# The change between two layer kinds of a fused graph network: another order on each engine in the last iterations, and chunk 1 entered inside the first half step

## What is computed

```
h = relu(layernorm(x)); x = x + attention0(h)              # 8 heads, masked by adj
h = relu(layernorm(x)); x = x + (o + layernorm(o)*gamma+beta), o = attention1(h)
h = relu(layernorm(x)); x = x + elu(att @ hw + beta*hw)    # hw = h W, att = softmax(leaky(s1+s2)*adj)
h = relu(layernorm(x)); 3 times:                           # gated recurrence
    a = adj @ h
    z = sigmoid(a W3 + h U3); r = sigmoid(a W4 + h U3)
    hv = tanh(a W5 + (r*h) U5);  h = (1-z) h + z hv
x = x + h
```

## Time and profile before

| | us |
|---|---|
| median of 3 runs (lowest to highest) | 1570.43 (1569.55 to 1574.69) |
| the profiled execution, its own time | 1572.46 |
| its span, first to last instruction | 1570.4 |
| PE busy / DVE busy / ACT busy / POOL busy | 1483.0 / 1243.8 / 993.3 / 534.6 |

### The profile page before, as it was taken

How to read it: one execution, slowest core, us unless ns; L and a number is a source line. 1 busy time by engine, 2 the same in 40 slices (tenths; PEclk the granted TensorE clock), 3 DMA queues, 4 the chain that set the end, 5 groups by cost and what they waited for, 6 DMA issues and landing times.

```text
span 1570.4 us, 45103 instructions
## 1 busy us (share of the span) xinstructions
PE 1483.0 (94%) x18552; PEld 1259.4 (80%) x18552; DVE 1243.8 (79%) x2511; ACT 993.3 (63%) x1793; POOL 534.6 (34%) x622
## 2 busy tenths in 40 slices
PE   3899999899999997699999999999999999999997
PEld 3789989799888886488788788788788788787885
DVE  3787887988899997588788788788788788888766
ACT  3676767667777775566666666666666566666553
POOL 1667767667788885311111111111101111111000
PEclk9999999999999999799999999999999999999999
DMA  9200000002233224100000000000000000000000
GB/s 255 84 3 0 0 0 1 16 16 43 56 59 74 53 55 56 28 1 1 28 1 1 29 1 1 29 1 1 28 1 1 28 1 1 28 2 1 28 2 27
DMA packets 36805, 40.86 MB, mean 26 GB/s; under 512 B 11840, under 2 KB 31808, under 8 KB 36672
## 3 DMA queue, kind: packets, MB, share of 16 engines
q0 software_dynamic: 4608, 16.78, 5.7%
q1 hardware_dynamic: 32064, 22.10, 5.0%
HBM read 13.71 MB, written 8.39 MB: 14 GB/s over the span
## 4 chain that ended last, share of the span: by engine, by line
PE 69%; DVE 16%; issue 5%; POOL 5%; ACT 4%; DMA 1%; SPq 0%; DVEq 0%; POOLq 0%; ACTq 0%
PE ring L99 32%; PE scores L99 22%; PE scores L1553 3%; PE ring L1347 2%; PE scores L1311 2%; DVE total L957 2%; POOL s L530 2%; PE ring L1512 2%; PE ring L1494 2%; PE ring L1384 1%; DVE hv L1186 1%; DVE hv L1184 1%; PE ring L1602 1%; DVE r L1225 1%; PE ring L1467 1%
## 5 line engine op out<-in xcount | busy, mean ns | idle before, releaser
L530 POOL TENSOR_TENSOR s<-s,mx 128x512 f32<-128x512 f32 x128 | 138.4, 1110 | 48.1 <-DVE mx L953 48.0
L536 POOL TENSOR_TENSOR s<-s,rtotal 128x512 f32<-128x512 f32 x128 | 131.5, 1058 | 36.4 <-DVE rtotal L959 36.2
L594 POOL TENSOR_TENSOR r_var_eps<-r_mean_var,eps 128x4 f32<-128x4 f32 x16 | 8.2, 510 | 371.1 <-DVE r_mean_var L1107 371.1
L669 ACT ACTIVATE s<-s 128x512 f32<-128x512 f32 x128 | 78.4, 642 | 77.6 <-POOL s L530 77.6
L1198 DVE TENSOR_TENSOR rhp_lo<-r,rhp_hi 128x1024 fp32r<-128x1024 f32 x48 | 58.8, 1226 | 70.6 <-ACT rhp_hi L816 70.6
L948 DVE SCALAR_TENSOR_TENSOR s<-scores,mask 128x512 f32<-128x512 f32 x128 | 87.0, 680 | 35.0 <-PE scores L1311 35.0
L808 ACT ACTIVATE later_w<-ring 128x512 f32<-128x512 f32 x64 | 34.8, 596 | 114.2 <-PE ring L1512 114.2
L841 ACT ACTIVATE hv<-scores,bias 128x512 f32<-128x512 f32 x96 | 66.2, 690 | 57.1 <-PE scores L99 57.1
L1206 DVE TENSOR_TENSOR agg_lo<-scores,agg_hi 128x512 fp32r<-128x512 f32 x96 | 61.8, 685 | 50.1 <-ACT agg_hi L835 49.6
L681 ACT ACTIVATE pT<-ring 128x512 f32<-128x512 f32 x128 | 66.1, 603 | 46.9 <-PE ring L1347 46.9
L859 ACT ACTIVATE r<-r,bias_half 128x512 f32<-128x512 f32 x96 | 64.3, 716 | 44.7 <-DVE r L1225 44.7
(11 more groups left out here) (295 smaller groups left out, 5170.3 us busy)
## 6 DMA issues: line engine op xcount, KB each, us to landing
x<-beta_less_one POOLq DMA_DIRECT2D x16, 512.0 KB, 4.6
x<-o POOLq DMA_DIRECT2D x16, 512.0 KB, 6.5
out_x<-x SPq DMA_DIRECT2D x16, 512.0 KB, 2.9
x<-in_x SPq DMA_DIRECT2D x1, 6656.0 KB, 30.4
later_w<-in_L_gnn_w_w SPq DMA_DIRECT2D x3, 512.0 KB, 6.8
x<-in_x SPq DMA_DIRECT2D x1, 1024.0 KB, 10.4
stage<-in_L_gnn_w_qkv SPq DMA_DIRECT2D x3, 256.0 KB, 3.1
x<-in_x SPq DMA_DIRECT2D x1, 512.0 KB, 4.0
```

The source lines that it names most:

```text
L530: pool.tensor_tensor(sr, sr, mx[:, r, :].unsqueeze(2).to_broadcast([P, CT * 2, N]), ALU.subtract).then_inc(s_shifted, 1)
L536: pool.tensor_tensor(sr, sr, rtotal[:, r, :].unsqueeze(2).to_broadcast([P, CT * 2, N]), ALU.mult).then_inc(p_ready, 1)
L669: act.activation(s[:, par, r, :, :, :], s[:, par, r, :, :, :], ACT.Exp).then_inc(p_exp, 1)
```

## The change

On each of the four engines the lines between the attention pipeline and the half steps stand in another order. Chunk 1's graph attention is transposed into and aggregated in banks of `ring` instead of `high`, its aggregation is issued by TensorE inside the first half step, between the `u3` and the adjacency product, and chunk 1 enters at that half step's end, after the `w5` product. The first half step has a program of its own (`begin`) on PE, ACT and DVE. `hw_next` lies in another part of SBUF. GpSimd's last pipeline step is written out, with `scale(T - 1)` behind the fourfold `normalise`. No operation is added or taken away. `agg_high`, `agg_low`, `r_sum`, `z_sum`, `r_tanh`, `adjacency`, `o_half`, `graph_read`, `graph_exp`, `graph_positive` and `graph_negative` are the old lines under names of their own.

```
         g_hT = Parts(plan, "g_hT", [P, FT, CW], start["hT_hi"])
         h0 = [sb("h0_a", [P, FT, CW], F32, start["qT"]), sb("h0_b", [P, FT, CW], F32, start["kT"])]
         r_hn = [sb(f"r_hn_{q}", [P, CT, D], F32, start["s"] + 4096 * n) for n, q in enumerate("ab")]
-        hw_next = sb("hw_next", [P, CT, WX], F32, start["s"] + 8192)
+        hw_next = sb("hw_next", [P, CT, WX], F32, start["pT"])
         hu = sb("hu", [P, FT, CW], F32, start["s"] + 8192)
         r = sb("r", [P, FT, CW], F32, start["s"] + 12288)
...
@@ -615,23 +615,32 @@
 
                 norms(-2, 0, 0)
                 iterations(pool, body)
-                body(T - 1, 1, 1)
+                norms(T - 1, 1, 1)
+                norm(gn, 1, 1)
+                for r in range(3):
+                    shift(T - 1, 1, r)
+                beta_to_x(T - 1, 1)
+                shift(T - 1, 1, 3)
+                o_to_x(T - 1, 1, 1)
                 pool.wait_ge(v_ready, T * 2)
                 pool.memset(adjT[:], 0.0).then_inc(adj_cleared, 1)
                 pool.memset(att[:], 0.0).then_inc(att_cleared, 1)
-                norms(T, 0, 1)
+                for r in range(R):
+                    normalise(T - 1, 1, r)
+                g_shift(0)
                 beta_to_x(T, 1)
                 o_to_x(T, 0, 1)
-                g_shift(0)
+                scale(T - 1, 1, 1)
+                norms(T, 0, 1)
+                norm(rn, 0, 0)
+                g_shift(1)
                 scale(T, 0, 1)
-                g_shift(1)
-                norm(rn, 0, 0)
                 norms(T + 1, 1, 1)
                 o_to_x(T + 1, 1, 1)
-                scale(T + 1, 1, 1)
-                norm(rn, 1, 1)
                 norms(T + 2, 0, 1)
                 o_to_x(T + 2, 0, 1)
+                norm(rn, 1, 1)
+                scale(T + 1, 1, 1)
                 scale(T + 2, 0, 1)
                 group(0)
                 with pool.Fori(1, GROUPS - 1) as g:
...
+                def begin(s):
+                    for m in range(FT):
+                        act.wait_ge(hu_ready, m + 1)
+                        act.activation(hu[:, m, :], ring[:, 2 + m, :], ACT.Copy).then_inc(hu_copied, 1)
+                    graph_read(1, ring, 0)
+                    agg_high(0)
+                    graph_exp(1)
+                    o_normalise(T + 1, 1, 1)
+                    o_normalise(T + 2, 0, 1)
+                    act.wait_ge(b_ready, 5)
+                    r_tanh(0)
+                    norm_rows(rn, r_hn[1], 1, 1)
+                    enter(1, 1)
+                    graph_normalise(2, 0)
...
                 graph_normalise(0, 0)
                 copy_pT(T - 1)
                 o_normalise(T - 1, 1, 1)
+                graph_high(0, high)
                 for q in range(R - 1):
                     exponential(T - 1, 1, q)
-                graph_high(0, high)
                 o_high(T - 2)
                 exponential(T - 1, 1, R - 1)
-                graph_normalise(1, 1)
                 for t in range(CT):
                     copy_hw(0, t, high, 2)
+                graph_normalise(1, 1)
                 copy_pT(T)
                 graph_high(1, high)
-                o_normalise(T, 0, 1)
                 g_exponential(0)
                 o_high(T - 1)
-                for t in range(CT):
-                    copy_hw(1, t, high, 0, hw_next)
+                copy_hw(1, 0, high, 0, hw_next)
+                copy_hw(1, 1, high, 0, hw_next)
                 graph_out(0, high, 2)
+                copy_hw(1, 2, high, 0, hw_next)
+                copy_hw(1, 3, high, 0, hw_next)
+                o_normalise(T, 0, 1)
+                norm_rows(rn, r_hn[0], 0, 0)
                 g_exponential(1)
-                norm_rows(rn, r_hn[0], 0, 0)
-                graph_out(1, high, 0)
                 enter(0, 0, high)
-                o_normalise(T + 1, 1, 1)
-                act.wait_ge(b_ready, 5)
-                norm_rows(rn, r_hn[1], 1, 1)
-                o_normalise(T + 2, 0, 1)
                 halves(act, half)
...
+                def begin(s):
+                    graph_positive(1, ring, 0)
+                    agg_low(0)
+                    graph_negative(1)
+                    recurrence_stats(1)
+                    r_sum(0)
+                    z_sum(0)
+                    rows_stats(gn, 2)
+                    final_sum(T + 2, 0, 1)
+                    enter(1, 1)
...
                 for q in range(3):
                     mask_and_max(T - 1, 1, q, 1)
                 take_first(T - 1, 1, 1)
+                graph_low(0, high)
                 mask_and_max(T - 1, 1, 3, 1)
                 take_out(T - 3, 1, 1, 1)
-                o_low(T - 2)
                 sums(T - 1, 1, 0)
                 sums(T - 1, 1, 1)
-                graph_low(0, high)
+                o_low(T - 2)
                 sums(T - 1, 1, 2)
                 sums(T - 1, 1, 3)
-                o_stats(T - 1, 1, 1)
-                final_sum(T - 1, 1, 1)
                 dve.tensor_scalar(beta_ident[:], ident[:], g_beta[:, 0:1], None, ALU.mult).then_inc(beta_ident_ready, 1)
                 graph_scores(0, high, 2)
+                final_sum(T - 1, 1, 1)
+                o_stats(T - 1, 1, 1)
+                dve.wait_ge(att_cleared, 1)
+                graph_attention(0)
                 graph_low(1, high)
+                dve.wait_ge(beta_ident_ready, 1)
+                copy_attT(0, high, 2)
                 take_first(T, 0, 1)
                 take_out(T - 2, 1, 0, 1)
-                dve.wait_ge(att_cleared, 1)
-                graph_attention(0)
                 o_low(T - 1)
-                dve.wait_ge(beta_ident_ready, 1)
-                copy_attT(0, high, 2)
-                graph_scores(1, high, 0, hw_next)
                 graph_out(0, high, 2)
                 recurrence_stats(0)
+                graph_scores(1, high, 0, hw_next)
+                o_stats(T, 0, 1)
                 take_first(T + 1, 1, 1)
                 take_out(T - 1, 1, 1, 1)
                 graph_attention(1)
-                copy_attT(1, high, 0)
+                enter(0, 0, high)
+                copy_attT(1, ring, 0)
                 final_sum(T, 0, 1)
-                graph_out(1, high, 0)
-                enter(0, 0, high)
-                o_stats(T, 0, 1)
-                recurrence_stats(1)
+                final_sum(T + 1, 1, 1)
                 o_stats(T + 1, 1, 1)
-                final_sum(T + 1, 1, 1)
-                dve.wait_ge(x_final, CHUNKS - 2)
-                halves(dve, first_half)
+                halves(dve, half)
...
+                def begin(s):
+                    pe.wait_ge(h0_lo_ready, FT)
+                    pe.wait_ge(x_done, T * 2)
+                    for m in range(FT):
+                        product(pe, ring[:, 2 + m, :], columns(wT["u3"], m), moving(hp[0])).then_inc(hu_ready, 1)
+                    graph_aggregate(1, ring, 0, hw_next)
+                    pe.wait_ge(e_sum, 2)
+                    pe.wait_ge(hw_copied, 2 * CT)
+                    pe.wait_ge(adj_loaded, 32)
+                    adjacency(r_hn[0])
+                    pe.wait_ge(agg_lo_ready, FT)
+                    pe.wait_ge(x_plus_pos, 4)
+                    for m in range(FT):
+                        product(pe, ring[:, m, :], columns(wT["w4"], m), moving(agg)).then_inc(r_ready, 1)
+                    for m in range(FT):
+                        product(pe, high[:, m, :], columns(wT["w3"], m), moving(agg)).then_inc(z_ready, 1)
+                    for m in range(FT):
+                        product(pe, high[:, 2 + m, :], columns(wT["w5"], m), moving(agg), ends=False)
+                    pe.wait_ge(hu_copied, FT)
+                    enter(1, 1)
...
                                                         h[s.other][:, f, t * P:(t + 1) * P], ident[:])
                             last.then_inc(final_ready, 1)
                     if not s.last:
-                        if not s.first:
-                            pe.wait_ge(hv_done, n * FT)
+                        pe.wait_ge(hv_done, n * FT)
                         for m in range(FT):
                             product(pe, high[:, 2 + m, :], columns(wT["w5"], m), moving(agg), ends=False)
 
                 iterations(pe, body)
                 scores_piece(T - 1)
                 p_transposes(T - 1, 1)
-                o_products(T - 1, 1)
+                o_half(T - 1, 1, 0)
                 pe.wait_ge(s_masked, (T - 1) * R + 2)
                 graph_rows(0, high)
+                o_half(T - 1, 1, 1)
                 values(T - 1, 1)
                 pe.wait_ge(g_hT_lo_ready, FT)
                 pe.wait_ge(gw_lo_ready, 2)
@@ -1628,17 +1701,17 @@
                 values(T, 0)
                 graph_attT(0, high, 2)
                 pe.wait_ge(g_hT_lo_ready, 2 * FT)
-                for t in range(CT):
-                    if t >= 2:
-                        pe.wait_ge(hw_copied, CT + t - 1)
+                graph_product(1, 0, high, 0)
```

(8 more changed lines are left out.)

207 lines of the change are left out of this document (110 added, 97 removed).

## The result

The changed kernel takes 1560.94 us, the median of five runs (1556.06 to 1561.42); the kernel before, run beside it, 1570.43 (1569.55 to 1576.07). The ratio of the runs is 0.9918, with a 95% interval of 0.9902 to 0.9933: 0.8% faster, and the median lies just inside the range (by 0.06 us). Two medians of five runs are a coarse measure: alone they give 0.9940, and beside the runs further down the same kernel before had medians of 1572.91 to 1575.31. About two thirds of the forecast gain are found in the profile (spans 1570.4 and 1558.6, so 11.8 us of 18.2) and half in the medians (9.5).

The account below looks back on a forecast made before the run. TensorE was bound by 25.8 us of idle time and 8.3 us of clock loss in a 71.81 us stretch. Cutting these to 14.1 and 2.6 gave 17.4, the walk 18.2: 1570.4 - 18.2 = 1552.2 us, range 1547 to 1561.

Parts of the forecast that it names:

- small-gain rival: Gain of only 8 to 15.5 us, through engine hand-offs and a slow clock at w4 or the second u3; chance 0.27.
- Two signs: Prediction wrong if w4 or the second u3 runs slow, or the part behind is no longer 904 us long.
- Step 1: Chunk 0's products: the 5.91 us stop and 1.65 us of slow clock go; 1.7 us of waits replace them.
- Step 2: Chunk 0's attention: att, excluded by GpSimd's scale, is ready at 608.2; TensorE waits 1.65 us.
- Steps 3 and 4: Up to chunk 0's entry, chunk 1's attention and u3: waits 1.1, 2.35, 1.8 and 0.7 us; u3 loses 2.63.
- Step 5: First half step: TensorE waits 2.05 us ahead of w4; w4, w3 and w5 take 2.8 to 2.95 us each.
- Step 6: Second half step: r_hn_b ready in time, the 8.88 us stop gone; final_sum(T + 2) comes last, a 2.75 us wait.
- ledger of idle time: TensorE's waits in the stretch from values(T - 1) to the second u3: 14.1 us against 25.8, 11.7 gained.
- Clock loss 2.6 against 8.3: Time lost to slow clock in the stretch up to the second half step's u3: 2.6 us against 8.3, 5.7 gained.
- Its operands for the rest are no later: After the second half step's u3 starts, inputs come no later than before, so nothing is lost there.

Follow-up runs that it names:

- chunk0_alone: Kernel before with only chunk 0's part of the change: transposes between the output product's halves, early high and low parts, earlier hw copies; 1571.65 us, ratio 0.9983.
- beta_early: Changed kernel with VectorE making beta_ident right after chunk 0's low parts, ahead of the last mask; 1557.34 us, ratio 0.9894 to the kernel before.
- scale_later: Changed kernel with scale(T - 1) behind the norms of T on GpSimd; 1554.21 us, ratio 0.9882 to the kernel before.
- norm_alone: Kernel before with only GpSimd's norm of chunk 1 moved ahead of scale(T + 1); 1570.98 us, ratio 0.9988.
- gpsimd_old_order: Changed kernel with GpSimd's last five calls back in the old order; 1563.29 us, ratio 0.9943 to the kernel before.
- sum_behind_low: Changed kernel with final_sum(T + 2) behind chunk 1's low parts on VectorE; 1560.83 us, ratio 0.9919 to the kernel before.
- fill_gaps: Changed kernel with 70 needless products, results overwritten, ahead of five of TensorE's waits; 1557.21 us, ratio 0.9888 to the kernel before.
- both_holds_fill: Changed kernel with early beta_ident, scale(T - 1) behind T's norms, and 36 needless products ahead of chunk 0's entry, chunk 1's attention transposes and w4; 1550.73 us, ratio 0.9854.
- both_holds: Changed kernel with beta_ident made ahead of the last mask and scale(T - 1) behind the norms of T; 1556.27 us, ratio 0.9889 to the kernel before.
- enter_before_w5: Changed kernel with chunk 1's entry transposes ahead of the w5 product instead of behind it; 1560.14 us, ratio 0.9904 to the kernel before.
- fill_w4: Changed kernel with 14 needless products only in the stop ahead of w4; 1557.32 us, ratio 0.9899 to the kernel before.
- holds_fill_enter: Same edits as both_holds_fill, plus chunk 1 entered ahead of the w5 product; 1554.05 us, ratio 0.9882 to the kernel before.

## Why the prediction was right in sign and range, and too large

The measured 1560.94 lies 0.06 us inside the edge of the range, and that it fell inside is luck. The gain of 11.8 us in the profile is not the forecast's 15.5 to 21, but that of the small-gain rival (8 to 15.5, chance 0.27). Two signs that the prediction had named for being wrong came true: `w4` and the second `u3` ran slow, and the part behind the stretch is 906.3 us long (1558.6 - 652.33) instead of 904.

**Step 1** held. The stop of 5.91 and the slow clock behind it went; the waits that took its place were 0.62 + 0.21 us, not 1.7. Taken by itself the step is worth 3.0 of the 13.6 us of the stretch (`chunk0_alone`).

**Step 2** had the mechanism, and 1.65 of the 2.81 us that TensorE waited. `att` ended 0.7 us behind the `scale`, as said, but at 609.55 instead of 608.2. About half of these 1.35 us is the later start of the `scale` (605.84 for 605.1). The working overlooked `beta_ident`, which it left at the 0.28 us of the trace before, where GpSimd had only operations on 4 columns under way; under `normalise` it takes 1.80. The other half is the `scale` itself, 2.99 us for the 2.37 of the earlier trace rows; it takes 3.00 in `beta_early` too, and why is not shown. `beta_early` and `scale_later` show both holds. The Trainium skill had this as well, in the very section that the step quotes (SBUF — State Buffer, "Who interferes with whom"): a `tensor_scalar` can read through both of VectorE's ports, and then contends with GpSimd although it has one input. The trace agrees: 1.80 us beside `normalise`, 0.28 apart from it.

**Steps 3 and 4** held in the idle time: 0.20 + 0.63 ahead of chunk 1's products and `s2` (1.1 forecast), 2.44 for the entry (2.35), 1.01 + 0.20 instead of 1.8 + 0.7. `u3` took 4.34 us at 0.63, not 5.42 at 0.50. That price, taken from the nearest row, is met in `scale_later` (5.22 at 0.51), so it is what can happen and not what always does.

**Step 5** held: one stop of 2.01 (2.05 forecast). But `w4` behind it was at 0.62 and lost 1.6.

**Step 6** held in its first part: the norm of chunk 1 follows its statistics at once, `r_hn_b` ends at 646.87 and is no longer waited for. `norm_alone` and `gpsimd_old_order` say what this rests on: not the queue of GpSimd alone, which took 0.9 us off the stop. That ScalarE's order and the entry's place are the other part is read from the waits in `norm_alone`; no run has either of them alone. Its second part was wrong in cause. The stop of 2.44 (2.75 forecast) is the entry's own round trip: four copies by ScalarE, then the low part. `final_sum(T + 2)`, named as the last comer, ends 0.8 us too early to matter (VectorE's timeline in the change), and `sum_behind_low` shows it.

```profile
648.59 1.21 DVE L1034 TENSOR_TENSOR x<-x,o_n 128x1024 f32<-128x1024 f32 x1
650.60 0.69 DVE L1208 TENSOR_TENSOR hp_b_lo<-ring,hp_b_hi 128x512 fp32r<-128x512 f32 x1 [0.81 <-ACT h_b L816]
```

**The sum.** The ledger of idle time was mis-sized by 1.5 in the safe direction (12.6 for 14.1). The step that failed is the other one, "Clock loss 2.6 against 8.3", which measures 7.3 to 7.9: only `u3` was charged (2.63), while more stages ran slow. Beside the same stages in `fill_gaps` the losses are: chunk 1's products 1.2 us, chunk 0's aggregation 1.0, the entry's transposes 0.6, the two sets of attention transposes 0.5 each, `u3` 1.5, `w4` 1.5. That is 4.7 to 5.3 us of the 6.4 missing from the profile. `fill_gaps` and `both_holds_fill` show that the time is real: with the stops filled the stretch is 4.9 and 3.0 us shorter, and for `both_holds_fill` beside `both_holds` the medians (5.5 us) and their intervals show it as well. The small-gain rival had this mechanism, on `w4` and the second `u3`, and its 10 us are nearer to the result than the forecast's 18.2. The clock can also spend what a shorter wait saves: step 1 alone brought chunk 0's attention 4.6 us forward and got 3.0.

**"Its operands for the rest are no later"** failed too, for 1.64 us: the next two half steps need 22.02 instead of 20.38. In the change that is the slow second `u3` exactly (1.65). But where it ran at full clock the two still needed 21.87 to 21.89, with waits for `g_hn` (0.34) and for a copy of `hw` (0.51) in its place: in `enter_before_w5` `g_hn`, behind GpSimd's two `scale`, was ready 59.40 us after `values(T - 1)`, against 59.35 in the change. The 0.3 us of the rest is within what the runs differ by (883.97 to 884.65 in most). Where it is 885.4 to 885.7, the last `u5` product ran at a low clock (last section).

Of the 8.7 us between 1552.2 and the median, 6.4 are thus in the profile; of the remaining 2.3, 2.0 are the difference of profiled execution and median in the kernel before, which the change does not have.

## What to carry to other kernels

When an order is changed so that one long stop becomes five short ones, keep the account of the clock stage by stage, and charge the stages behind each stop of about 2 us as possibly slow: here stops of 2.0 to 2.8 us were followed by stages that lost 1.2 to 1.7 us each, though not every time. Take from the trace what the neighbour engine does during an operation before its duration is carried to a new place; a short one beside GpSimd's long ones may take the length of theirs. And follow a wait that is taken away to the end of the kernel: 2.0 us off the stop ahead of chunk 0's attention came with 4.6 in the stretch and 4.4 at the end of that profile, while of the 1.3 us that the earlier entry took off the last stop nothing is found at the end. That the first stop of a chain is always the better one to remove is not shown by two runs with such clocks.

## What was not expected of the hardware

The length of a stop alone does not decide whether the next stage is slow. Stops and granted clock of the stage behind, from the windows above and, for the last rows, those below:

| stage | stop ahead | granted clock |
|---|---|---|
| `w4`, the change | 2.01 | 0.62 |
| `w4`, scale_later | 2.01 | 1.00 |
| second `u3`, both_holds_fill | 2.66 | 0.62 |
| second `u3`, fill_w4 | 2.63 | 1.00 |
| chunk 1's products, before | 1.81 | 1.00 |
| chunk 1's products, chunk0_alone | 2.72 | 0.62 |
| last `u5` of the kernel, the change | 1.78 | 1.00 |
| last `u5` of the kernel, enter_before_w5 | 1.78 | 0.63 |

The last `u5` product stands some 890 us behind the edits, in code that no variant alters. Its windows in the change and in `enter_before_w5`:

```profile
1544.31:1547.38 3.07, 3.06 (x12) 2.18 (x12) 0.57 (x1) 0.69 (x1) 0.00 (x0) 1.00 0.00 0
```

```profile
1547.92:1552.53 4.61, 4.61 (x12) 3.35 (x12) 1.27 (x2) 0.69 (x1) 0.00 (x0) 0.63 0.00 0
```

It takes 4.61 or 4.62 us at 0.63 in the profiles of `enter_before_w5`, `fill_gaps`, `fill_w4` and `holds_fill_enter`, and 3.06 or 3.07 at 1.00 in all the others. A part of the 1.55 us is taken up by the wait behind it; from the last transposes of `h_a` to those of `h_b` these four need 13.19 to 13.42 us and the change 12.37. They are also the four, of those with the new order, whose second `u3` ran at full clock. One profile of each does not show whether the one follows from the other.

The low clock need not begin with the stage either: in the change the second and third product of `w4` start 0.23 us apart (639.15 and 639.38), those from 639.71 to 642.70 0.43 apart. What besides the stop decides it, the runs do not settle. In these runs needless products that filled most of a stop were followed by a stage at 1.00 each time.

And a GpSimd operation on only 4 columns took 1.96 us instead of 1.04 in `norm_alone`, while VectorE's last sum (1.19 us, two inputs in SBUF) ran beside it, as the shift of the scores took 1.53 instead of 0.61 in the change: the holding goes both ways.
